# Image attention: probabilities turned by DMA transposes instead of TensorE, and the transfers of queries, keys and values issued by ScalarE

## The reference, cut to what matters

```python
q = norm(norm(x)) @ Wq            # 512 x 64 per head
k, v = keys and values of the 512 image tokens and the 154 context tokens (666 rows)
p = softmax(q k^T / 8)            # 512 x 666
out = p @ v                       # 512 x 64
x = x + tanh(gate) * (concat of heads) @ Wo
```

## Time and profile before

| | us |
|---|---|
| median of 3 runs | 1660.23 (1658.74 to 1662.96) |
| the profiled execution | 1667.16 |
| its span, first to last instruction | 1665.3 |
| granted clock of TensorE, mean over the span | 0.937 |
| busy in the span: TensorE, VectorE, ScalarE, GpSimd | 1445.0, 1110.9, 780.5, 877.9 |

### The profile page before, as it was taken

How to read it: one execution, slowest core, us unless ns; L and a number is a source line. 1 busy time by engine, 2 the same in 40 slices (tenths; PEclk the granted TensorE clock), 3 DMA queues, 4 the chain that set the end, 5 groups by cost and what they waited for, 6 DMA issues and landing times.

```text
span 1665.3 us, 36883 instructions
## 1 busy us (share of the span) xinstructions
PE 1445.0 (87%) x13680; PEld 985.4 (59%) x13849; DVE 1110.9 (67%) x2918; ACT 780.5 (47%) x1566; POOL 877.9 (53%) x1308
## 2 busy tenths in 40 slices
PE   5999999999999897977888889979977777789987
PEld 3777777777777775755566555534544344434545
DVE  5889788878777773544764667854446567487753
ACT  4777667767766661632233355554234434211111
POOL 5789889978776693363335653422033332153330
PEclk8999999999999999998899899999987979789998
DMA  7333232111221111250000000000000000000000
GB/s 279 103 90 86 86 97 50 49 44 45 61 49 44 52 51 57 58 182 1 1 1 1 9 9 1 2 1 1 1 1 1 0 1 1 1 1 1 7 7 14
DMA packets 35479, 64.31 MB, mean 39 GB/s; under 512 B 7535, under 2 KB 25042, under 8 KB 34147
## 3 DMA queue, kind: packets, MB, share of 16 engines
q1 hardware_dynamic: 33831, 59.83, 12.2%
q0 software_dynamic: 1472, 2.12, 0.4%
HBM read 30.64 MB, written 12.66 MB: 26 GB/s over the span
## 4 chain that ended last, share of the span: by engine, by line
PE 35%; DVE 10%; ACT 4%; POOL 3%; issue 2%; DVEq 0%; ACTq 0%; POOLq 0%
PE banks L520 9%; PE banks L2210 3%; PE banks L2196 2%; PE banks L3058 2%; PE banks L3001 1%; PE banks L2723 1%; PE banks L2717 1%; PE banks L2163 1%; PE banks L495 1%; DVE work L2293 1%; PE banks L2199 1%; PE banks L1763 1%; PE banks L305 1%; PE banks L2985 1%; PE banks L1687 1%
## 5 line engine op out<-in xcount | busy, mean ns | idle before, releaser
L1059 POOL TENSOR_TENSOR work<-work 128x512 bf16<-128x512 f32 (+1 forms) x512 | 358.7, 723 | 76.4 <-ACT work L952 75.5
L835 DVE TENSOR_REDUCE work<-banks 128x1 f32<-128x666 f32 x256 | 216.4, 846 | 64.9 <-PE banks L752 62.2
L959 ACT ACTIVATE work<-banks,work 128x666 f32<-128x666 f32 x256 | 208.1, 813 | 30.3 <-DVE work L835 23.3
L952 ACT ACTIVATE work<-banks 128x512 f32<-128x512 f32 x256 | 152.8, 597 | 146.0 <-PE banks L763 145.7
L460 POOL TENSOR_TENSOR norm_room<-norm_room,minus_half 128x4 f32<-128x4 f32 (+1 forms) x56 | 53.1, 949 | 294.7 <-DVE norm_room L435 170.0
L763 PE MATMUL banks<-const,work 128*128 128x128 f32 x1024 | 159.2, 278 | 15.5 <-ACT work L952 12.3
L752 PE MATMUL banks<-work 128*128 128x154 bf16 (+1 forms) x898 | 160.4, 295 | 9.7 <-DVE work L909 1.6
L520 PE MATMUL banks<-work,weights_b 128*128 128x512 bf16 (+1 forms) x830 | 150.1, 337 | 13.6 <-ACT work L1348 7.0
L752 PEld LDWEIGHTS banks<-work 128*128 128x128 bf16 x1024 | 96.0, 98 | 80.6 <-DMA work<-work 2.8
L2293 DVE TENSOR_REDUCE work<-banks 128x2 f32<-128x308 f32 x192 | 87.0, 472 | 82.0 <-PE banks L2163 56.2
L791 PE MATMUL banks<-work 128*128 128x65 bf16 (+1 forms) x3840 | 136.6, 192 | 3.0 <-POOL work L1059 1.8
(11 more groups left out here) (463 smaller groups left out, 3294.7 us busy)
## 6 DMA issues: line engine op xcount, KB each, us to landing
work<-work SPq DMA_DIRECT2D x128, 166.5 KB, 2.8
sorted<-in_pads SPq DMA_DIRECT2D x10, 838.5 KB
weights_b<-in_weights SPq DMA_DIRECT2D x1, 4120.0 KB, 13.4
work<-scratch SPq DMA_DIRECT2D x64, 64.0 KB, 1.9
weights_b<-in_weights SPq DMA_DIRECT2D x1, 2824.0 KB, 12.3
weights_a<-in_weights SPq DMA_DIRECT2D x1, 2056.0 KB
weights_a<-in_weights SPq DMA_DIRECT2D x1, 2050.0 KB, 9.9
work<-work SPq DMA_DIRECT2D x32, 64.0 KB, 1.9
```

Source lines behind the costliest of these rows:

```text
L835: ve.tensor_reduce(self.neg_max[i % 4], self.slot[i % 2][:, 0:KEYS0], AX_X, ALU.max, negate=True).then_inc(self.mark("max"))
L952: ac.activation(self.probs_t[u % 2][:, h, 0:4, j * P:(j + 1) * P], self.bank_a.rearrange("p (t n) -> p t n", t=4), ACT.Copy).then_inc(self ...
L959: ac.activation(self.probs[i % 3], self.slot[i % 2][:, 0:KEYS0], ACT.Exp, bias=self.neg_max[i % 4]).then_inc(self.mark("exp"))
L1059: po.tensor_tensor(parts[:, :, :, 0], exact, parts[:, :, :, 1], ALU.subtract).then_inc(self.mark(event, i - 3))
```

## The change

Exponentials are no longer turned by TensorE. GpSimd makes the low halves directly in the row of exponentials (now 704 words wide, the last 38 zero; four buffers instead of three), and SyncE issues one DMA transpose per step: the buffer, seen as 1,408 bf16 columns by 128 partitions, becomes 11 blocks (`WORDS0`) of 128 partitions by 128 queries. In such a block partition 2m holds the low half of key m, partition 2m + 1 its high half. There are six such destination buffers (`TURNS`); a transpose waits until the weighing of six steps back is done. An exponential waits until the transpose of four steps back has landed.

Because high and low of a key now lie on neighbouring partitions, the values have to lie there doubled. They are first kept by rows (`v_rows`) and then copied by six transfers per group to even and odd partitions of `v`. A weighing has 11 blocks by 2 products of 65 and 64 columns per step. The gathered rests with all that belongs to them (`rest`, `ctx_last`, `four_times_po`, `rest_due`) go.

The transfers of queries, keys and values stand in one function `image_heads`. For group 0 SyncE calls it, ahead of the load of the expert weights. For all other groups ScalarE does, behind its work of the step: two query transfers in step 2 of the group before, the third in step 3, four of keys in step 6, six of values in step 0 of the group itself. The pads are issued by SyncE in step 5 of ten groups, ahead of that step's transpose.

The diff, cut to its core:

```diff
+HALF_KEYS = P // 2
+WORDS0 = -(-KEYS0 // HALF_KEYS)
+TURNS = 6
...
     def image_memory(self):
...
-        self.v = [self.place(KT0 + 1, 2, 2 * VALUE, dt=BF16).rearrange("p t s (h d) -> p t s h d", h=2) for _ in range(3)]
-        self.probs = [self.place(KEYS0) for _ in range(3)]
+        self.v = [self.place(WORDS0, 2, 2 * VALUE, dt=BF16) for _ in range(3)]
+        self.v_rows = self.place(KT0, 2, 2 * VALUE, dt=BF16)
+        self.v_heads = self.v_rows.rearrange("p t s (h d) -> p t s h d", h=2)
...
-        self.probs_t = [self.place(2, KT0 - 1, 2 * P) for _ in range(2)]
-        self.rest, self.rest_t = ([self.place(P) for _ in range(2)] for _ in range(2))
-        self.ctx_last = self.place(2, P + 32, dt=BF16)
+        self.probs = [self.place(WORDS0 * HALF_KEYS) for _ in range(4)]
+        self.probs_t = [self.place(WORDS0, P, dt=BF16) for _ in range(TURNS - 2)]
+        image_at, self.work_at = self.work_at, 0
+        self.probs_t += [self.place(WORDS0, P, dt=BF16) for _ in range(2)]
...
-    def image_turn_pe(self, pe, i):
+    def image_turn_pe(self, pe, u):
+        ps = self.bank(pe, 5, "mixed", u + 1)
+        pe.wait_ge(*self.at("divided", u + 1))
+        for j in (0, 1):
+            m = pe.transpose(ps[:, j * P:(j + 1) * P], self.divided[:, 2 * j:2 * j + 2, :].rearrange("p h d -> p (h d)"), self.eye)
+        m.then_inc(self.mark("mix_turned"))
+
+    def turned_in(self, sub):
+        return self.at(f"dma_turn{sub % TURNS}", 16 * (sub // TURNS + 1))
+
+    def values_in(self, n):
+        return self.at("dma_values", 96 * (n + 1))
...
     def image_weigh_pe(self, pe, u, h):
...
-        orders = ((0, 1, D0 + 1), (0, 0, D0 + 1), (1, 1, D0))
         for j in (0, 1):
-            for t in range(KT0 - 1):
-                for which, (of_values, of_probs, width) in enumerate(orders):
-                    pe.matmul(self.out_heads[:, 2 * j + h, 0:width], parts[:, h, t, j * P:(j + 1) * P, of_probs], v[:, t, of_values, h, 0:width],
...
+            sub = 4 * u + 2 * h + j
+            pe.wait_ge(*self.turned_in(sub))
+            for t in range(WORDS0):
+                for part, width in ((0, D0 + 1), (1, D0)):
+                    m = pe.matmul(self.out_heads[:, 2 * j + h, 0:width], self.probs_t[sub % TURNS][:, t, :], v[:, t, part, h, 0:width],
...
     def image_ve(self, ve):
...
-            if 2 <= i < SUBS + 2:
...
-                ve.tensor_copy(self.probs_t[u % 2][:, h, 4, j * P:(j + 1) * P], self.bank_b[:, 0:P]).then_inc(self.mark("kept_b", i - 2))
-            u = self.rest_due(i)
...
     def image_ac(self, ac):
...
-            if 2 <= i < SUBS + 2:
...
-                ac.activation(self.probs_t[u % 2][:, h, 0:4, j * P:(j + 1) * P],
-                              self.bank_a.rearrange("p (t n) -> p t n", t=4), ACT.Copy).then_inc(self.mark("kept_a", i - 2))
             if i < SUBS:
-                if i >= 3:
-                    ac.wait_ge(*self.at("turned_b", i - 1))
-                    ac.wait_ge(*self.at("gathered", i - 3))
+                if i >= 4:
+                    ac.wait_ge(*self.turned_in(i - 4))
...
             if i // 8 + 1 < GROUPS0 and i % 8 in (0, 2, 4, 6):
                 self.image_keep_ac(ac, i // 8 + 1, i % 8 // 2)
+            n = (i - 1) // 8 + 1
+            if i % 8 in (2, 3, 6, 0) and 1 <= n < GROUPS0:
+                self.image_heads(ac, n, (2, 3, 6, 0).index(i % 8))
...
     def image_po(self, po):
...
             if 1 <= i < SUBS + 1:
...
-                po.tensor_copy(self.rest[u % 2][:, 32 * (2 * j + h):32 * (2 * j + h + 1)], self.probs[(i - 1) % 3][:, KEYS0 - 32:]).then_inc(self.mark("gathered", i - 1))
+                po.tensor_tensor(self.halves(whole)[:, :, 0], whole, self.halves(whole)[:, :, 1], ALU.subtract).then_inc(self.mark("low_a", i - 1))
...
     def image_sp(self, sp):
         self.loads(sp)
+        for which in range(4):
+            self.image_heads(sp, 0, which)
+        self.load_weights(sp, 1)
+        for i in self.image_steps():
+            n = (i - 1) // 8 + 1
+            if i % 8 == 5 and 2 <= n < 2 + PAD_PARTS:
+                self.pads_sp(sp, n - 2)
+            if 1 <= i < SUBS + 1:
+                sub = i - 1
+                if sub >= TURNS:
+                    sp.wait_ge(*self.at("weighed", (sub - TURNS) // 2 + 1))
+                sp.wait_ge(*self.at("low_a", sub))
+                sp.dma_start_transpose(self.probs_t[sub % TURNS], self.probs[sub % 4].bitcast(BF16)).then_inc(self.mark(f"dma_turn{sub % TURNS}", n=16), 16)
+
+    def image_heads(self, eng, n, which):
         top, bottom = slice(0, D0), slice(D0, 2 * D0)
...
+        if which == 0:
+            eng.wait_ge(*self.at("q_low", n + 1))
+            eng.dma_start(q[top, 1, :], q[bottom, 0, :]).then_inc(self.mark("dma_swap", n=16), 16)
+            eng.dma_start(q[bottom, 1, :], low[bottom, :]).then_inc(self.mark(f"dma_head{n % 2}1", n=16), 16)
+        elif which == 1:
+            eng.wait_ge(*self.at("dma_swap", 16 * (n + 1)))
+            eng.dma_start(q[bottom, 0, :], low[top, :]).then_inc(self.mark(f"dma_head{n % 2}0", n=16), 16)
+        elif which == 2:
+            eng.wait_ge(*self.at("k_low", 2 * n + 2))
             for h, own in ((0, top), (1, bottom)):
                 for half in (top, bottom):
+                    eng.dma_start(k[half, h, :, :], self.k_parts[own, :, :]).then_inc(self.mark(f"dma_head{n % 2}{h}", n=16), 16)
+        else:
+            eng.wait_ge(*self.at("v_low", 3 * n + 3))
+            if n >= 3:
+                eng.wait_ge(*self.at("weighed", 2 * (2 * n - 4)))
+            for word in (0, 1):
+                for h, own in ((0, top), (1, bottom)):
+                    eng.dma_start(v[word::2, h:WORDS0 - 1:2, :, :], rows[own, 0:KT0 - 1, :, :]).then_inc(self.mark("dma_values", n=16), 16)
+                eng.dma_start(v[word:2 * CTX_REST:2, WORDS0 - 1, :, :], rows[0:CTX_REST, KT0 - 1, :, :]).then_inc(self.mark("dma_values", n=16), 16)
```

More of the change, by code:

```diff
@@ L686, in image_pe @@
                 self.image_weigh_pe(pe, u, h)
[L687 to L688 removed]
+            if self.mix_due(i) is not None:
+                self.image_turn_pe(pe, self.mix_due(i))
             for what, b, _ in self.image_chores(i):
@@ L989, in image_keep_ac @@
             if part == 2:
[L990 to L993 removed]
+                if n >= 1:
+                    ac.wait_ge(*self.values_in(n - 1))
+                v = self.v_heads
+                for rows, tile, src in self.value_pieces():
                     ac.activation(v[rows, tile, 0, :, 0:D0], side[rows, src].rearrange("p (h d) -> p h d", h=2), ACT.Copy).then_inc(self.mark("v_kept"))
         else:
[L996 removed]
+            ac.activation(self.v_heads[:, 0:QT, 0, :, 0:D0], side.rearrange("p (t h d) -> p t h d", t=QT, h=2), ACT.Copy).then_inc(self.mark("v_kept"))
     def image_po(self, po):
```

156 lines of the change are left out of this document (30 added, 126 removed).

## The result

The changed kernel takes 1945.07 us (1936.91 to 1952.06, four runs), the kernel before 1659.49 in the same comparison: a ratio of 1.173 (95% interval 1.166 to 1.179), 286 us slower. The forecast of 1697 had the direction and one eighth of the size; the time lies outside the range of 1605 to 1810.

The account below looks back on a forecast made before the run. TensorE was taken to bound the kernel; afterwards a chain through ScalarE's key issues would. Terms +37 (chain), -18 (side work), +10 (pads) and +8 (start) gave +37 us: 1697 median, forecast's own range 1665 to 1735, whole range 1605 to 1810.

Parts of the forecast that it names:

- the start: First transpose queued behind the expert weights, delaying the fifth exponential from 37.0 to near 45 us: +8, bounds 3 and 12.
- the pads: Ten 838 KB transfers ahead of transposes on SyncE, mostly hidden by four probability buffers: 1.0 us each, +10, bounds 0 and 2.8.
- the DMA engines' time: Engines busy 2.3 us a step, as full as TensorE before; transpose 1.45 us; only 0.3 us a group charged for key delays.
- ScalarE's issues: Thirteen DMA issues a group on ScalarE, 0.55 us each, 7.2 a group, delaying the exponentials behind each burst.
- The second rival: Transposes become the bound once one costs over 1.5 us of all engines: 2.65 us a step, 1773 us; chance 0.22.
- Its sign: What would show the second rival: exponentials waiting for transposes at every step.
- Its other form: A transpose holds SyncE's queue over 2.35 us; a hold of 2.8 gives 1773 us; 0.06 of the second rival's chance.
- Exponential 6 to 8: Chain through key issue, landing, scores and maximum in each group: 6.5 us for two steps, within a group of 18.8.
- first rival: Not slower: ScalarE's issues disappear beneath running activations and TensorE's relief reaches the end; 1623 us, chance 0.33.
- GpSimd's low half: GpSimd makes the low part in one operation of 666 columns: 1.30 us a step, and doesn't end last.
- TensorE at full clock: TensorE's products costed at the old kernel's times, 0.030 us per narrow product, a weighing of 44 taking 1.32 us.
- The -18 for side work in new waits: Half of TensorE's side work (37 us in all) vanishes into its new waits: -18 us.

Follow-up runs that it names:

- plain_early: Changed kernel with plain copies for transposes, SyncE issuing all queries, keys and values, and keys issued in step 5 instead of 6: 1676.5 us, ratio 1.013.
- sp_heads: Changed kernel with the transfers of queries, keys and values issued by SyncE ahead of that step's transpose, none by ScalarE: 1867.1 us, ratio 1.126.
- plain: Changed kernel with each transpose replaced by a plain, unturned copy of the same 352 KB: 1796.9 us, ratio 1.084.
- filled: Changed kernel with sixteen idle 512-column products on TensorE ahead of each group's first scores, from the second group on: 1923.9 us, ratio 1.164.

## Why the prediction was wrong, step by step

**Accounted for.** Undone one after the other: a single queue -67 us, ScalarE's hold -11 (together 1945 to 1867), plain copies for transposes -163 (to 1704), keys a step earlier -27 (to 1677). In the stage these are 56, 5, 157 and 28 of 272 us. In another order the parts would be others (plain copies first: -148, then the queue -26 and the hold -67). plain_early is left with 1.3% (0.9 to 1.8) over the kernel before. Of that stage 27 us are left, and they lie in the first 88 steps: 2.78 us each against 2.32, 40 us, which are the start and the pads. Behind them plain_early needs 2.29 us a step against 2.37, 13 us less than before.

**The step that failed: the DMA engines' time, put down as hidden.** It wasn't in the sum at all: engines busy 2.3 us of a 2.35 us step were put down as fitting, and the only charge was "a fifth of one before each key transfer", 0.3 us. Three errors lie in it. A transpose costs 1.72 us of all engines, not 1.45, within its bounds (1.00 to 1.8). The rates were taken from stretches with one queue, and from two queues the same bytes take longer (16% more of the engines' time in the changed kernel than in sp_heads), which no row of before showed and no bound covered. And "as full as TensorE is now" was read as no cost. With the engines full the landings were longer: keys 4.6 instead of 2.8 us, transposes 5.6 against the assumed 4. The measured 1.72 alone makes the prediction's own sum 2.57 us a step, 0.22 over the 2.35; the rest up to 3.42 lies in the second queue, the longer landings, ScalarE's issues and the pads.

**The pads** were charged 1.0 us each, +10, with 2.8 as the upper bound. Steps 16 to 88, where they move, took 3.84 us each in the changed kernel and those behind them 3.19: 47 us, 4.7 for each of the ten, an estimate from these rows (in the kernel before both parts take 2.35 to 2.37). It fits the engines' rate: 838 KB at 175 GB/s are 4.9 us. So the four buffers hid hardly any of it. No run leaves the pads out.

**The second rival** named the mechanism: over 1.5 us a transpose the engines set the pace. With transposes at 1.72 us the engines were full, with plain copies at 0.92 they were not; the threshold itself was not tried. With bounds of 1.00 and 1.8 this rival deserved more than 0.22. Its price was too low: 2.65 us a step by the parts, 3.42 measured (3.19 behind the pads). Its sign, exponentials waiting for transposes at every step, came only in part, 46.6 us in 22 places; it shows in full where ScalarE doesn't issue (sp_heads, 220.6 us in 128). Its other form, SyncE's hold, was not it: in sp_heads the median hold is 1.62 us, and in the changed kernel 2.21 because its queue is full, below 3.42 either way.

**Exponential 6 to 8.** The chain was right and so was its place: scores wait for the keys once a group. The wait was to be 2 to 3 us and is 7; four key transfers hold the queue 3.8 us in the group shown, where the second was to be issued at 0.60 and landed 2.8 later.

**ScalarE's issues: between forecast and first rival.** The first rival said that they disappear beneath the activation. They do begin beneath it (510.38 exponential, 510.44 issue), but the two keys behind hold the queue 2.61 us and the next exponential waits 2.65 for "issue". In step 0 the six values hold it from 520.20 to 526.22, 1.0 us each where 0.55 was taken. Their medians, 0.64 and 0.86, are those of the same transfers on SyncE for group 0 (0.63 and 0.88), so that much is the transfer's own; single issues are longer, up to 2.25 here, and up to 2.16 in plain too. The rival's 1623 was reached by no kernel, not even by plain_early, which issues nothing on ScalarE and turns nothing. But its relief is there: the 0.08 us a step that plain_early gains behind the pads are about what this rival had (0.7 us a group).

**Right to the point:** GpSimd's low half, 1.304 us for 1.30. The direction. Near: the start, where the fifth exponential of after began at 48.39 for a forecast of 45 (3 to 12 over 37.0; it is 11.4), where the prediction had put it, in a wait for a transfer:

```profile
48.39 0.82 ACT L917 ACTIVATE work<-banks,work 128x666 f32<-128x666 f32 x1 [13.03 <-DMA work<-work]
```

**TensorE at full clock** was taken for every product; it got 0.79 to 0.85. Two weighings of after, of 44 narrow products each, behind a pause and in mid group:

```profile
502.52 2.27 PE L785 MATMUL banks<-work 128*128 128x65 bf16 x44
...
510.45 1.47 PE L785 MATMUL banks<-work 128*128 128x65 bf16 x44
```

The granted clock is 0.59 in the first stretch and 1.00 in the second. The second is near the 1.32 us of the forecast, the first isn't. The part of the clock that filled gave back was worth 10 to 21 us. The -18 for side work in new waits can't be seen beside such a loss.

## What to carry to other kernels

Before handing a resident turn to the DMA engines, add up the bytes of a step, by the rate of that very transfer, and treat a resource that would be 98% full as the new bound, not as hidden. Where the rate of a new kind of transfer is only bounded and the upper bound passes the step, that is the forecast. A transfer that is hidden only because the engines have room, as the pads were, has its full price once they have none. And keep transfers in one queue, off an engine whose next instruction is on the path: with full engines the queue that ScalarE opened cost more (67 of 78 us), with engines that had room ScalarE's time did (67 of 93).

## What the runs showed of the hardware

- A transpose of 11 blocks between places on the chip runs at 210 GB/s, half of the same bytes copied (393), with the engines full in both cases; its packets are small (379,056 of 449,615 packets of the program are under 512 bytes, 14,516 of 117,838 with plain copies).
- Two hardware queues, SyncE's and ScalarE's, took 15 to 22% more time for the same bytes than the parts one after the other, at a share near 1, where one queue with transposes and keys took 5% more. Inside the kernel two queues took 16% more of the engines' time with transposes and 3% with plain copies, at a share of 0.65 to 0.81. The Trainium skill (DMA: Bandwidth & Descriptors, section Rules for kernel authors) says that spreading transfers over engines gives no bandwidth and only saves the time to issue; the runs agree that it gives none, and show that with full engines it takes some.
- A transpose holds SyncE's queue 1.3 us at least, 1.62 to 2.21 in the median, against 0.54 for a plain copy of the same bytes: about the time that it takes the engines.
- An issue can hold its queue for several times its median: ScalarE's keys up to 3.1 us with the engines full (median 0.74) and 2.4 with room (0.63), where SyncE's never took over 1.13 before (0.60).
